# Second attention: the early masks and scores of unit v+2 put ahead of the turned maxima of unit v+1

## What is computed

```python
q = (x @ wq).reshape(b, s, H, HD)          # H = 32 heads, HD = 16
k = (x @ wk).reshape(b, s, H, HD)
v = (x @ wv).reshape(b, s, H, HD)
q = _apply_rotary(q, cos, sin)
k = _apply_rotary(k, cos, sin)
scores = jnp.einsum('bqhd,bkhd->bhqk', q, k) * scale
scores = jnp.where(causal[None, None], scores, jnp.finfo(scores.dtype).min)
probs = jax.nn.softmax(scores, axis=-1)
out = jnp.einsum('bhqk,bhkd->bqhd', probs, v).reshape(b, s, d)
return out @ wo
```

## Time and profile before

| | us |
|---|---|
| median of 3 runs | 1957.11 (1956.24 to 1957.84) |
| the profiled execution | 1959.17 |
| its span, first to last instruction | 1957.4 |
| outside the span | 1.8 |
| second attention, first to last turned maxima | 1569.8 to 1801.3 |

### The profile page before, as it was taken

One profiled execution on the slowest core, in us unless ns is written; L12 is line 12 of the kernel. 1 busy time (PEld: TensorE's weight loads), 2 busy tenths in 40 slices (PEclk: granted clock), 3 DMA queues, 4 the chain that ended last, 5 costly groups with the idle time before them and its releaser, 6 DMA issues.

```text
span 1957.4 us, 42259 instructions
## 1 busy us (share of the span) xinstructions
PE 1875.7 (96%) x14296; PEld 1618.5 (83%) x14296; DVE 1510.5 (77%) x2385; ACT 918.1 (47%) x2297; POOL 906.0 (46%) x872
## 2 busy tenths in 40 slices
PE   8999979999999999999999999998999979998997
PEld 3688869999999999999999999987798956666786
DVE  2577757878788787887877878788888658889876
ACT  1233334444444444444444444454654457888333
POOL 0133354444444444444444444355386557888111
PEclk9999989999999999999999999999999989999999
DMA  9577751111111111111111111221377776553121
GB/s 340 182 233 246 235 162 49 48 49 47 40 42 48 49 48 48 48 40 40 48 48 48 49 48 41 87 91 52 101 232 229 224 229 186 165 168 113 40 64 60
DMA packets 201841, 211.30 MB, mean 108 GB/s; under 512 B 19083, under 2 KB 172683, under 8 KB 200749
## 3 DMA queue, kind: packets, MB, share of 16 engines
q1 hardware_dynamic: 200836, 209.53, 34.6%
q10 hardware_dynamic: 936, 0.85, 0.1%
HBM read 128.40 MB, written 73.53 MB: 103 GB/s over the span
## 4 chain that ended last, share of the span: by engine, by line
PE 72%; issue 12%; DVE 8%; POOL 3%; DMA 2%; SPq 2%; ACT 1%; DVEq 0%; POOLq 0%; ACTq 0%
PE ps L1040 18%; PE ps L1001 18%; PE ps L1015 7%; PE ps L1029 4%; PE ps L1052 4%; DVE f_neg_max L1987 4%; PE ps L1803 3%; PE ps L1024 3%; PE ps L2603 2%; POOL k_rot L574 2%; PE ps L2567 2%; PE ps L2161 2%; PE ps L1813 1%; SPq L1303 1%; PE ps L2140 1%
## 5 line engine op out<-in xcount | busy, mean ns | idle before, releaser
L1040 PE MATMUL ps<-wo,ot 128*128 (+1 forms) x1536 | 388.4, 401 | 0.1
L1040 PEld LDWEIGHTS ps<-wo,ot 128*128 128x128 f32 x1536 | 281.1, 189 | 60.8 <-issue 1.2
L1001 PE MATMUL ps<-ht_hi,wq 128*128 (+1 forms) x2048 | 287.6, 283 | 5.4 <-DVE q_swap L873 5.4
L1001 PEld LDWEIGHTS ps<-ht_hi,wq 128*128 128x128 f32 x2048 | 268.4, 192 | 11.2 <-DVE q_swap L873 5.6
L799 ACT ACTIVATE prob<-ps,neg_max 128x128 f32<-128x128 f32 (+1 forms) x512 | 208.2, 420 | 129.8 <-DVE neg_max L880 104.8
L958 POOL TENSOR_TENSOR q_rot<-q_rot,q_swap 128x512 f32<-128x512 f32 x128 | 164.9, 1288 | 198.2 <-DVE q_swap L873 193.6
L806 ACT ACTIVATE pt<-ps 128x512 fp32r<-128x512 f32 x192 | 107.7, 597 | 302.0 <-PE ps L1052 302.0
L953 POOL TENSOR_TENSOR prob<-prob,inv_sum 128x512 f32<-128x512 f32 x64 | 66.6, 1040 | 280.9 <-DVE inv_sum L889 280.9
L1001 PE MATMUL ps<-ht_lo,wq 128*128 (+1 forms) x1024 | 165.0, 284 | 0.0
L1015 PE MATMUL ps<-pt,vv 128*128 128x512 f32 x576 | 145.5, 396 | 4.0 <-issue 3.7
L574 POOL TENSOR_TENSOR k_rot<-k_rot,k_swap 128x512 f32<-128x512 f32 x32 | 60.2, 1881 | 192.3 <-DVE k_swap L479 192.3
(11 more groups left out here) (247 smaller groups left out, 4128.1 us busy)
## 6 DMA issues: line engine op xcount, KB each, us to landing
stack_dram<-e_part SPq DMA_DIRECT2D x192, 128.0 KB, 2.4
v_dram<-v_part SPq DMA_DIRECT2D x32, 512.0 KB, 5.5
k_dram<-k_part SPq DMA_DIRECT2D x64, 256.0 KB, 2.5
kk<-k_dram SPq DMA_DIRECT2D x128, 128.0 KB, 2.1
vv<-v_dram SPq DMA_DIRECT2D x128, 128.0 KB, 2.1
f_q<-stack_dram SPq DMA_DIRECT2D x124, 104.0 KB
f_k<-stack_dram SPq DMA_DIRECT2D x124, 104.0 KB
wmod<-in_wmod SPq DMA_DIRECT2D x12, 1024.0 KB, 12.0
```

The costliest lines, as they stand in the source:

```text
L1001: mm = nc.tensor.matmul(ps_q[j][:, e], w[:, c:c + HD0], r[:, bass.ds(u % B, 1), k].rearrange("p o s -> p (o s)"), start=(n == 0), stop=(n ...
L1040: mm = nc.tensor.matmul(ps_y[j][:], o[:, j, h * P:(h + 1) * P], w[:, bass.ds(at + h * D, D)], start=(n == 0), stop=(n == len(passes) - 1))
```

## The change

On TensorE, the early masks and scores of v+2 are taken out from behind the shifted scores of v and put at the head of step v, ahead of the turned maxima of v+1. They now wait for VectorE's early maxima of v+1 (which read `s0`) and, in their place, for the exponentials of v-1 (which read `t1` in the same banks). The early masks now open their banks anew (`True` in place of `False`). The shifted scores no longer wait for `p_exp` except in the last steps. On VectorE, the early maxima of v+2 wait in addition for the far shifted scores of v, which write the same banks. The other engines are as they were.

```diff
     def vector(dve, side):
-        def maxima(u, first):
+        def maxima(u, first, at):
+            if at >= 0:
+                dve.wait_ge(t_done, 4 * u - 4)
             for t, sc in ((0, s0), (1, s1)):
                 dve.wait_ge(s_done, 4 * u + 2 * t + 2)
...
         def step(v, slot, at):
             if at < U - 2:
-                maxima(v + 2, slot % 2)
+                maxima(v + 2, slot % 2, at)
...
         def step(v, slot, at):
+            if 0 <= at < U - 2:
+                pe.wait_ge(smax, 2 * v + 3)
+                if at > 0:
+                    pe.wait_ge(p_exp, 2 * v)
+                put_masks(0, True)
+                scores_early(pe, v + 2, (slot + 2) % NS)
             if 0 <= at < U - 1:
                 turn_max(pe, v + 1, (slot + 1) % 2, at)
             if 0 <= at < U:
                 pe.wait_ge(m_out, 2 * v + 2)
-                if at > 0:
+                if at >= U - 2:
                     pe.wait_ge(p_exp, 2 * v)
                 shifted_near(v, slot)
                 shifted_far(v, slot)
-                if at < U - 2:
-                    put_masks(0, False)
-            if 0 <= at < U - 2:
-                scores_early(pe, v + 2, (slot + 2) % NS)
             if 0 <= at < U - 2:
                 scores_late(pe, v + 2, (slot + 2) % NS)
```

## The result

The changed kernel takes 1960.8 us (median of 22 runs, 1955.98 to 1964.06), the kernel before 1956.78 us (22 runs, 1952.54 to 1962.8). The ratio is 1.0019, 95% interval [1.0011, 1.0027]: a little slower, by 0.11 to 0.27%, on the edge of the 0.2% that the prediction takes as the least it can tell from no change. The forecast was 1959.7 us, with a range of 1953.5 to 1964.0. The profiled execution took 1960.25 us (span 1958.5); that of before 1959.17 (span 1957.4).

The account below looks back on a forecast made before the run. Before the change a ring of waits through VectorE set the step, afterwards TensorE and ScalarE at 3.33 us. Terms of -0.7 + 2.8 + 0.5 = +2.6 us on 1957.1 gave 1959.7 us, range 1953.5 to 1964.0.

Parts of the forecast that it names:

- two load waits: Steps 8 and 14: late keys now hold up everything queued on TensorE; 1.4 us each, +2.8 us.
- What bounds the kernel: Second attention before the change: no engine full; a ring of waits through VectorE's late maxima sets the 3.34 us step.
- TensorE's own ring: Changed step, turned maxima to turned maxima through ScalarE's copy, with no wait for VectorE: 3.33 us against 3.34.
- The gain in the even steps: Second attention: 0.01 to 0.02 us less in each of 49 steps, -0.7 us.
- The layout step: TensorE's change from 64-row tiles to matmuls using all 128 rows: 0.10 us, one more per step than before.
- VectorE's own ring: VectorE's own work in a changed step: between 3.17 and 3.33 us, taken as 3.2.
- The new wait on t_done is free: VectorE's early maxima: far shifted scores are done 0.4 us before the old wait on `s_done` let go.
- The last attention steps: From 1777 to 1801 us VectorE is the bound at 3.97 us a step and its work stays: 0 us.
- The start: Step 3: the head now waits for the far exponential of step 2, delaying the turned maxima: +0.5 us, at least 0.
- no further waits for keys: Apart from steps 8 and 14 the loads have 0.6 us of room: 0, at most 0.3 us a step.
- the load at the head costs more: Rival: after either load wait the next turned maxima follow the release by over 6 us; 1963.1 us, chance 0.23.
- VectorE becomes the bound: Rival: TensorE's ring falls to 3.05 us and VectorE's 3.18 decides the step; 1952.6 us, chance 0.14.

Follow-up runs that it names:

- experiment 4: In each order, an unread 4x32 activation added ahead of ScalarE's first copy of the turned maxima: 1954.23 us in the order of before, 1964.47 in the changed order.
- experiment 2: Kernel before with only the early masks moved to the head of the step, early scores left behind the shifted scores: 1953.94 us, ratio 0.9985.
- strewn pair: Both orders with the last phase's 1 MB loads cut into 256 KB pieces over later units, small tables behind: 1952.97 us (before), 1952.57 us (changed).
- experiment 5: Both orders with the last phase's 1 MB loads cut into 256 KB pieces behind later units, small tables after: 1952.97 us (before), 1952.57 us (changed).
- experiment 3: In each order, an unread write of 128x128 zeros on VectorE between early and late maxima: 1963.39 us in the order of before, 1958.93 in the changed order.
- masks_head: Kernel before with only the early masks moved to the head of the step, early scores left in their old place: 1953.94 us, ratio 0.9985.
- three strewn ones: Kernels with the last phase's loads cut and spread over later units: order of before 1952.97 us, changed order 1952.57, early masks alone at the head 1946.86.
- before_spread: Kernel before with the last phase's 1 MB loads cut into 256 KB pieces over later units, small tables behind them: 1952.97 us, ratio 0.9976.
- masks_spread: Kernel before with only the early masks at the head of the step and the last phase's loads cut and spread over later units: 1946.86 us, ratio 0.9951.

## Why the prediction was right, and where it was lucky

The forecast, "TensorE and ScalarE bound the step at 3.33 us, the two load waits cost 1.4 each", held in its first half, and its time is 1.1 us from the median. Of the second half the sum came out and the split did not, and a term of 1.3 us was not in the forecast at all. Term by term:

- **What bounds the kernel.** VectorE's late maxima, by the chain. Right: an added 0.17 us on VectorE lengthens the old step and not the new one.
- **TensorE's own ring, 3.33 us.** Right to 0.02. By the timeline above: turned maxima to the late masks 1.06 (forecast 1.05), late masks and scores 0.56 (0.56), values 1.23 (1.21), early masks and scores 0.50 (0.51), together 3.35. The link that mattered, the bare copy of ScalarE, is shown by experiment 4 from one side and by experiment 2 from the other.
- **The gain in the even steps, -0.7 us.** It was +0.1 in the 39 steps: 3.347 against 3.344. That is the 0.02 by which the ring was short, times 49; nothing else failed.
- **The layout step, 0.10 us.** The masks at the head take 0.32 to 0.33 us in the chain where they come behind the values' 32-column tiles, 0.23 behind the shifted scores and 0.24 behind the scores. That is 0.09 for one such step. The forecast had its 0.10 from the last eight matmuls of the values, 0.32 with the turned maxima behind them, and the eight before them, 0.22 (1662.85 to 1663.07). That the change of layout is what takes this time was my estimate from these rows; no run changes the layout alone. The second such step of the forecast, from the early scores to the turned maxima, can't be told apart in them, so no run shows that part of the ring's sum.
- **VectorE's own ring, 3.2 us.** Only bounded by the runs: TensorE's 3.17 with one step in four at 3.30, at the loop's end, came to 3.200 with VectorE not on the path, so VectorE can follow at 3.17, the lower of my two bounds.
- **"The new wait on t_done is free".** It is the last wait of VectorE's early maxima (0.20 us for L2163), but VectorE was off the path, so it cost nothing. No run leaves this wait out. The early maxima came at 1.15 us behind the turned maxima instead of 1.05.
- **The last attention steps, 0 us.** They took 0.3 us less.
- **The start, +0.5 us.** Mean +0.6 for begin to T7 (and +0.7 in the strewn pair). It shows in two places: 0.5 at step 0, half of it given back in the next, and at step 3, where the turned maxima come 1.00 us behind the far exponential (1590.83, with 1589.23 + 0.60 for its end) instead of 0.50 as in the earlier trace rows. The mean itself is within the scatter: from "begin" to T7 the five traces with the order of before and the loads in place took 34.4 to 37.0 us. And the forecast of no further waits for keys missed one: both traces of the changed kernel have one at the head of step 2, 0.40 and 0.33 us, which no trace of before has.

```profile
1589.23 0.60 ACT L2053 ACTIVATE f_prob<-ps 128x512 f32<-128x512 f32 x1 [4.14 <-DVE f_neg_max L1989]
...
1590.83 0.59 PE L2142 MATMUL ps<-ident,f_neg_max 128*4 128x128 f32 x2
```

- **The two load waits, +2.8 us.** The sum is near (+2.5 for steps 7 to 16 by the table, 2.2 by experiment 5), the way to it only by half. At step 14 the step in which everything queues behind the keys costs +1.4, as worked out, with 5.20 us to the next turned maxima where I had said 4.5 to 5, and 2.67 us of idle time where I had said over 3. At step 8 the trace that I read had a wait that other executions of the same kernel have not: over all five traces with the order of before and the loads in place (three unedited, two with a dummy), steps 7 to 10 took 0 to 4.4 us more than three even steps, and over four of the changed order 0.4 to 3.1. The means, 2.2 and 2.1, don't differ. There the change costs nothing that I can show; the +1.5 of the table is within the scatter of single executions. A term of 1.4 was booked on a wait that one trace showed by chance. Over the same five and four traces steps 13 to 16 differ by 1.8 us (2.4 and 4.2 us above three even steps), so what the loads cost the change is at step 14. The queueing as such is there at step 8 too when the keys are late: in the two traces of the changed kernel the next turned maxima follow the release by 5.13 and 4.86 us, against 3.55 before. The 1.4 us a wait was my choice between two bounds: by the granted clock of 0.69, 62% of the stretch behind the second wait ran at 0.50 and the rest at 1.00, the only two levels in the traces. And one reading was loose: the loads do not come late by a shared queue both times, since at step 14 SyncE asks for them late (experiment 5).
- **Missing from the sum: the last phase, +1.3 us.** I had taken the work from T62 on as unchanged. It is, in instructions, but not in clock (0.86 and 0.72 over 12 us, in the last section). That this stood in for the step-8 term, whose 1.4 us do not show over all the traces, is the luck in the forecast.

The rival "the load at the head costs more" asked for over 6 us from release to the next turned maxima; it was 5.20, with one stretch of the lower clock behind each wait, 3.4 us at 0.50 behind the one at step 14, so it fell. Its time of 1963.1 us, on which the upper end of the range leans, was my estimate; no run of the changed order shows the further loss behind each wait that it counts on. "VectorE becomes the bound" fell by experiment 3.

## What to carry to other kernels

When a block is taken out of the ring that bounds a loop, ask what it was hiding where it stood: the early masks could go, the early scores couldn't, since they covered ScalarE's copy. Half of the move (masks alone) brings 0.15%, the whole of it costs 0.19%. Work whose operands may be late should not stand at the head of a step, where all later work of its engine waits with it: at step 14 the next turned maxima came 5.20 us behind the release instead of 3.13. The better cure for such waits was to take away what delays the loads: here large transfers ahead of them, and an engine busy issuing small ones, which the experiments moved together. And one trace shows one execution: a wait for a transfer that is 1.9 us in it can be 0 in the next.

## What was not expected of the hardware

**The granted clock in the last phase differs between kernels that do the same work there.** Stretches of 12 us near the end, of the kernel before and then of the changed kernel (columns as in rows 1):

```profile
1936.00:1948.00 12.00, 9.94 (x41) 7.78 (x42) 7.46 (x16) 2.20 (x4) 2.36 (x1) 0.86 0.12 45
```

```profile
1937.00:1949.00 12.00, 11.08 (x40) 8.94 (x41) 6.62 (x18) 1.07 (x2) 2.34 (x1) 0.72 0.13 46
```

The same work at a mean clock of 0.86 and of 0.72: 3.4 of the 12 us at a clock of 0.50 in the one and 6.7 in the other ((1 - 0.86) x 2 x 12 and (1 - 0.72) x 2 x 12). In the traces that have only this longer stretch, T62 to the end is 0.9 to 1.4 us longer than before. It isn't tied to the order of the second attention: all three traces of the kernel before and `masks_head` show the shorter stretch, the changed kernel, the four kernels with an added write or activation and the three strewn ones the longer. `masks_head`, `before_spread` and `masks_spread` have in addition a stretch of the lower clock at the beginning of the phase; the last two, which have both, have the longest last phase (158.98 and 159.11 us). This is the row of `before_spread`, at 0.72 over 6 us:

```profile
1799.00:1805.00 6.00, 5.48 (x40) 4.07 (x44) 2.94 (x6) 2.77 (x5) 3.28 (x4) 0.72 0.00 0
```

What decides between the shorter and the longer stretch stays open: no experiment moved it on its own. In these runs edits ahead of this phase came with 0.9 to 2.8 us more in it than the kernel before has.
